# Router logits with Wr stationary in four column strips, the fourth Gram transpose as its own step, and batch 2's exponential and groups two or three places later

## The reference

```python
x = x + layernorm(attn(layernorm(x), Wqk, Wv, Wo, tau))
x = x + layernorm(ffn(layernorm(x), ln_g, ln_b, Wr, W1, W3, W2, W1s, W3s, W2s))
```

```python
logits = h @ Wr                                # h [8192, 256], Wr [256, 7]
top_vals, top_idx = jax.lax.top_k(logits, 2)
gates = jax.nn.softmax(top_vals, axis=-1)
# each token goes to its two experts, at most 732 places an expert, in order of tokens
routed = ...                                   # (silu(xe @ W1) * (xe @ W3)) @ W2, times the gate
shared = silu(h @ W1s) * (h @ W3s) @ W2s
```

## Time and profile before

| | |
|---|---|
| median of 3 runs | 1165.59 us |
| lowest and highest | 1161.06, 1172.66 us |
| the profiled execution | 1164.55 us |
| its span in the trace | 1162.8 us |
| TensorE busy | 1082.8 us, 93% |
| VectorE busy | 660.4 us, 57% |
| ScalarE busy | 506.2 us, 44% |
| GpSimd busy | 384.4 us, 33% |
| records of `u_route`'s products (line 1245) | 256 |

### The profile page before, as it was taken

One profiled execution on the slowest core, in us unless ns is written; L12 is line 12 of the kernel. 1 busy time (PEld: TensorE's weight loads), 2 busy tenths in 40 slices (PEclk: granted clock), 3 DMA queues, 4 the chain that ended last, 5 costly groups with the idle time before them and its releaser, 6 DMA issues.

```text
span 1162.8 us, 19459 instructions
## 1 busy us (share of the span) xinstructions
PE 1082.8 (93%) x6837; PEld 988.9 (85%) x6837; DVE 660.4 (57%) x1712; ACT 506.2 (44%) x887; POOL 384.4 (33%) x344
## 2 busy tenths in 40 slices
PE   6889889999989999869999889999999999999994
PEld 6877778998777898758898679999999999999873
DVE  6767555566844567744468423455453644546596
ACT  3334234343243343334344323546464554635385
POOL 3114360113460112450112561243353444311276
PEclk9989999999989999989999899999999999999998
DMA  9872360143350043352134230453241424315589
GB/s 306 326 250 98 121 199 2 37 142 122 119 182 19 19 143 134 106 182 73 37 109 129 105 104 17 156 124 102 63 138 35 135 55 116 82 14 158 201 192 218
DMA packets 83310, 141.44 MB, mean 122 GB/s; under 512 B 10389, under 2 KB 57625, under 8 KB 83233
## 3 DMA queue, kind: packets, MB, share of 16 engines
q1 hardware_dynamic: 64736, 105.11, 27.5%
q0 software_dynamic: 18496, 35.35, 12.9%
HBM read 73.72 MB, written 66.69 MB: 121 GB/s over the span
## 4 chain that ended last, share of the span: by engine, by line
PE 77%; DVE 8%; issue 5%; POOL 3%; ACT 2%; another core or an unknown queue 2%; DMA 1%; DVEq 0%; POOLq 0%; SPq 0%; ACTq 0%
PE bank L1115 23%; PE bank L1117 23%; PE bank L1116 23%; PE bank L1132 2%; POOL out_dram L890 2%; PE bank L1245 2%; POOL sb_t_scale L895 1%; PE bank L1234 1%; DVE sb_act_lo L1666 1%; PE bank L1277 1%; PE bank L1159 1%; DVE sb_act L1690 1%; DMA sb_ysb<-in_L_ffn_W2s_dram 1%; PE bank L1187 1%
## 5 line engine op out<-in xcount | busy, mean ns | idle before, releaser
L1690 DVE TENSOR_TENSOR sb_act<-bank,sb_act 128x512 f32<-128x512 f32 (+2 forms) x240 | 148.7, 620 | 397.2 <-PE bank L1117 301.0
L1115 PE MATMUL bank<-sb_h_hi,sb_wup_lo 128*128 128x512 f32 (+2 forms) x960 | 357.8, 373 | 8.0 <-ACT sb_act L1044 4.8
L1117 PE MATMUL bank<-sb_h_hi,sb_wup_hi 128*128 128x512 f32 (+2 forms) x960 | 352.5, 367 | 1.5 <-issue 1.5
L1116 PE MATMUL bank<-sb_h_lo,sb_wup_hi 128*128 128x512 f32 (+2 forms) x960 | 352.4, 367 | 0.0
L1044 ACT ACTIVATE sb_act<-bank 128x512 f32<-128x512 f32 (+2 forms) x240 | 129.8, 541 | 434.5 <-PE bank L1117 324.4
L1115 PE MATMUL bank<-sb_wdn_hi,sb_act_lo 128*128 128x256 f32 (+1 forms) x848 | 248.1, 293 | 17.4 <-DVE sb_act_lo L1666 10.5
L1116 PE MATMUL bank<-sb_wdn_lo,sb_act_hi 128*128 128x256 f32 (+1 forms) x848 | 240.0, 283 | 1.7 <-issue 1.7
L1117 PE MATMUL bank<-sb_wdn_hi,sb_act_hi 128*128 128x256 f32 (+1 forms) x848 | 240.5, 284 | 0.3 <-issue 0.3
L1115 PEld LDWEIGHTS bank<-sb_h_hi,sb_wup_lo 128*128 128x128 f32 x960 | 182.8, 190 | 27.8 <-ACT sb_act L1044 5.1
L1117 PEld LDWEIGHTS bank<-sb_h_hi,sb_wup_hi 128*128 128x128 f32 x960 | 182.3, 190 | 23.6 <-issue 0.5
L1116 PEld LDWEIGHTS bank<-sb_h_lo,sb_wup_hi 128*128 128x128 f32 x960 | 183.0, 191 | 18.5 <-issue 1.0
(11 more groups left out here) (248 smaller groups left out, 1289.0 us busy)
## 6 DMA issues: line engine op xcount, KB each, us to landing
sb_xin<-in_L_ffn_W_dram SPq DMA_DIRECT2D x28, 512.0 KB
sent_scratch<-sb_early SPq DMA_DIRECT2D x8, 1548.0 KB, 9.0
sb_x<-in_L_attn_x_dram SPq DMA_DIRECT2D x16, 512.0 KB
out_dram<-sb_x SPq DMA_DIRECT2D x16, 512.0 KB, 3.9
sb_xin<-in_L_attn_x_dram SPq DMA_DIRECT2D x14, 512.0 KB
sb_xin<-in_x_turned_dram SPq DMA_DIRECT2D x14, 512.0 KB, 4.1
y_scratch<-sb_ysb SPq DMA_DIRECT2D x14, 512.0 KB
sb_xn<-in_L_ffn_W_dram SPq DMA_DIRECT2D x14, 512.0 KB
```

Of the source, the lines that this page charges most:

```text
L1115: t_.matmul(o, a_lo, b_hi, start=start, stop=False, skip_group_check=True)
L1116: t_.matmul(o, a_hi, b_lo, start=False, stop=False, skip_group_check=True)
L1117: return t_.matmul(o, a_hi, b_hi, start=False, stop=stop, skip_group_check=True)
L1690: v.tensor_tensor(act[:, m % 2, 0:c.w], bank[(4 if c.wide and m % 2 else 0) + 1][:, 0:c.w], act[:, m % 2, 0:c.w], ALU.mult).then_inc(act_o ...
```

## The change

The logits: Wr is kept in 32 columns, 25 of them zero (a memset by POOL ahead of the other constants; SP's load of Wr waits for it). It is the stationary operand now, and h moves: for each half k of the channels and each of four strips of 32 output partitions, one product with 128 moving columns, the strip's 32 tokens of each of the group's 4 tiles. The result has experts on 32 partitions a strip, so VectorE's copy becomes a transpose in 32x32 blocks, into a tile `lgq` of 32 columns a token tile, of which `lg` is a view of 7.

The chain: the fourth transpose leaves `m_turn` for a step `m_cross` in the next place, together with `m_sym`; what follows moves one place. Batch 2's exponential moves three places, what is behind it with it, and its groups two (`MIX_AT` 107 in place of 105), with their routing and sends.

```diff
-        wr = sb("wr", [P, KC, E])
+        wr = sb("wr", [P, KC, QUAD])
...
-        lg = sb("lg", [P, 2 * GT, E])
+        lgq = sb("lgq", [P, 2 * GT, QUAD])
+        lg = lgq[:, :, 0:E]
...
-        logits = bank[7][:, 0:GT * 8].rearrange("p (t e) -> p t e", e=8)[:, :, 0:E]
+        turned_logits = bank[7][:, 0:GT * QUAD]
...
-        M_STEPS = ("m_gram", "m_turn", "m_sym", "m_times_wqk", ...
+        M_STEPS = ("m_gram", "m_turn", "m_cross", "m_sym", "m_times_wqk", ...
...
-        M_AT_PLACES = (0, 1, 1, 2, 2, 3, 3, 4, 5, 5, 6, 7, 8, 8, 9, 9, 10)
+        M_AT_PLACES = (None, (0, 1, 2, 2, 3, 3, 4, 4, 5, 6, 6, 7, 8, 9, 9, 10, 10, 11),
+                       (0, 1, 2, 2, 3, 3, 4, 4, 5, 6, 6, 9, 10, 11, 11, 12, 12, 13),
+                       (0, 1, 2, 2, 3, 3, 4, 4, 5, 6, 6, 7, 8, 9, 9, 10, 10, 11))
...
-        X_AT, MIX_AT = (None, 14, 72, 131), (None, 46, 105, 164)
+        X_AT, M_AT, MIX_AT = (None, 14, 72, 131), (None, 34, 93, 152), (None, 46, 107, 164)
...
-            put(b, MIX_AT[b] - 12, 0, zip(M_STEPS, M_AT_PLACES))
+            put(b, M_AT[b], 0, zip(M_STEPS, M_AT_PLACES[b]))
...
-            weight(wr, Wr, vec_in)
+            sp.wait_ge(const_ok, 1)
+            sp.dma_start(wr[:, :, 0:E], Wr.rearrange("(k p) n -> p k n", p=P)).then_inc(vec_in, 16)
...
+            made(v.memset(wr[:, :, :], 0.0))
...
                                      ident[:, :])
+
+            def m_cross(b, q):
+                if b > 0:
                     pe.wait_ge(m_chain, b * 9 + 1)
                 o = 0 if b == 0 else D
                 t_.transpose(bank[6][:, o:o + P], gf[:, 0, P:D], ident[:, :]).then_inc(m_pe, 1)
...
-                for t in range(GT):
-                    for k in range(KC):
-                        ins = t_.matmul(bank[7][:, t * 8:t * 8 + E], h[:, k, t * P:(t + 1) * P], wr[:, k, :],
+                for k in range(KC):
+                    for quad in range(0, P, QUAD):
+                        ins = t_.matmul(bank[7][quad:quad + QUAD, 0:GT * QUAD].rearrange("p (t r) -> p t r", r=QUAD),
+                                        wr[:, k, :],
+                                        h[:, k, :].rearrange("p (t r) -> p t r", r=P)[:, :, quad:quad + QUAD],
                                         start=(k == 0), stop=(k == KC - 1))
...
-                v.tensor_copy(lg[:, q % 2 * GT:(q % 2 + 1) * GT, :], logits).then_inc(lg_ok, 1)
+                v.transpose(lgq[:, q % 2 * GT:(q % 2 + 1) * GT, :].rearrange("p t r -> p (t r)"),
+                            turned_logits).then_inc(lg_ok, 1)
```

More of the change, by code:

```diff
@@ L73, in sandwich_kernel @@
     CLEAR = 4
+    QUAD = 32
     SENT_ROWS = 32 * SPARE * P
@@ L212, in sandwich_kernel @@
         blank = early[:, 0:SPARE * UW]
-        lg = sb("lg", [P, 2 * GT, E])
+        lgq = sb("lg", [P, 2 * GT, QUAD])
+        lg = lgq[:, :, 0:E]
         same = sb("same", [P, 2 * GT, E])
@@ L338, in sandwich_kernel @@
         t_out = [sem(f"t_out{i}") for i in range(TY)]
-        NCONST = 21
+        NCONST = 22
         H_LOADS = 16 * (GB - 1)
@@ L444, in sandwich_kernel @@
         T_STEPS = (("x_turned", (13, 16, 18, 20)), ("x_keep", (16, 18, 21, 23)), ("x_low", (17, 19, 22, 24)))
-        M_STEPS = ("m_gram", "m_turn", "m_sym", "m_times_wqk", "m_keep_t", "m_dots", "m_keep_s", "m_diag", "m_rowdiag",
+        M_STEPS = ("m_gram", "m_turn", "m_cross", "m_sym", "m_times_wqk", "m_keep_t", "m_dots", "m_keep_s", "m_diag", "m_rowdiag",
                    "m_logits", "m_exp", "m_softmax", "m_times_wo", "m_keep_n", "m_times_wv", "m_high", "m_low")
@@ L448, in sandwich_kernel @@
                       ("x_turned", (14, 14, 14, 15)), ("x_keep", (16, 18, 24, 26)), ("x_low", (19, 20, 34, 34)))
-        M_FIRST_AT = (20, 22, 23, 24, 25, 26, 27, 28, 30, 31, 32, 33, 34, 35, 36, 36, 37)
-        M_AT_PLACES = (0, 1, 1, 2, 2, 3, 3, 4, 5, 5, 6, 7, 8, 8, 9, 9, 10)
+        M_FIRST_AT = (20, 22, 22, 23, 24, 25, 26, 27, 28, 30, 31, 32, 33, 34, 35, 36, 36, 37)
+        M_AT_PLACES = (None, (0, 1, 2, 2, 3, 3, 4, 4, 5, 6, 6, 7, 8, 9, 9, 10, 10, 11),
+                       (0, 1, 2, 2, 3, 3, 4, 4, 5, 6, 6, 9, 10, 11, 11, 12, 12, 13),
+                       (0, 1, 2, 2, 3, 3, 4, 4, 5, 6, 6, 7, 8, 9, 9, 10, 10, 11))
         O_STEPS = (("o_mix", 0), ("o_stats", 1), ("o_norm", 3), ("o_apply", 3), ("o_add", 5), ("u_stats", 7),
@@ L1263, in u_count @@
                 ins.then_inc(r_cnt, 1)
-            steps = {"x_gram": x_gram, "m_turn": m_turn,
+            steps = {"x_gram": x_gram, "m_turn": m_turn, "m_cross": m_cross,
                      "m_times_wqk": m_times_wqk, "m_dots": m_dots, "m_rowdiag": m_rowdiag,
@@ L1585, in top @@
                 of_e = rank[:, :].rearrange("p (a e) -> p a e", a=1).broadcast_to([P, 2 * GT, E])
-                ch.link(v.tensor_reduce(best[:, c, :], lg[:, :, :], AX.X, ALU.max))
-                ch.link(v.tensor_tensor(same[:, :, :], lg[:, :, :], over_e(best[:, c, :]), ALU.is_equal))
+                ch.link(v.tensor_reduce(best[:, c, :], lg, AX.X, ALU.max))
+                ch.link(v.tensor_tensor(same[:, :, :], lg, over_e(best[:, c, :]), ALU.is_equal))
                 ch.link(v.tensor_tensor(same[:, :, :], same[:, :, :], of_e, ALU.mult))
@@ L1595, in r_top @@
                 ch.link(top(0, ch))
-                v.scalar_tensor_tensor(out=lg[:, :, :], in0=oh[:, :, 0, :], scalar=-BIG, in1=lg[:, :, :],
+                v.scalar_tensor_tensor(out=lg, in0=oh[:, :, 0, :], scalar=-BIG, in1=lg,
                                        op0=ALU.mult, op1=ALU.add).then_inc(r_top_ok, 1)
```

## The result

The changed kernel took 1157.68 us in the median of 21 runs (1147.87 to 1171.18). The kernel before, run beside it, took 1163.20 us (21 runs, 1157.01 to 1176.55). The ratio is 0.994, 95% interval 0.9912 to 0.9968: about 7 us gained, less than 1% (5.5 us by the two medians). The forecast's parts summed to 14.1 us gained, its time to 1150.0 us; the time lies in its range of 1138 to 1164. The profiled execution took 1158.23 us, its span 1156.5 us.

A forecast was written before the change was run, and what follows sets the result against it. TensorE was taken as the bound through the middle of batch 1, busy all of a 90 us stretch. 1164.55 - 6.0 (logits) - 4.2 (fourth transpose) - 3.9 (batch 2 later) = 1150.45, so 1150.0 us; range 1138 to 1164.

The forecast's parts named there:

- the wait ahead of batch 2's fourth transpose: Sign on TensorE: at most 3.5 us, with a down or an up between the third and fourth transpose.
- the waits ahead of the product with Wo: Sign at L1179: about 1 us in batches 1 and 3, none in batch 2.
- The logits: Router logits on TensorE: a group falls from 1.70 to 1.2 us, saving 0.5 us; 6.0 us gained in all.
- 16 records in 9 steps: Logits on TensorE: only a strip's second record overlaps the next strip's first, so the records take 0.9 us.
- The rival of full overlap: Logits: all four strips run at once, saving 1.3 us a group, 15.6 in all; around 1141 us, chance 0.15.
- Twelve groups by the step: Only batches 1 to 3's groups count, where TensorE is the bound: 12 x 0.5 = 6.0 us gained.
- VectorE's transpose: Replaces VectorE's copy of the logits: 0.28 us, 0.1 us more, 16 times, covered by VectorE's free time.
- The fourth transpose: Own step in the attention chain: 0.8 + 1.5 + 4.5 gained, 2.6 lost at L1179; 4.2 us gained.
- likely to stay at its place: Batch 1, VectorE ahead of L1453: the 7.07 us gap stays; a down fills TensorE's hole, 0.8 us gained.
- part 3: Batch 2's exponential three places later, groups two: L1179's 2.1 us wait goes, clock adds 0.9 twice; 3.9 us gained.
- the clock: Batch 2, TensorE around L1179: idle time also cost clock speed; 0.9 us gained twice.
- The sends: Rival: batch 2's moved sends put two more unreleased waits into batch 3's chain, 4 to 9 us; about 1157, chance 0.10.

The follow-up runs named there:

- gated_after: Changed kernel with POOL waiting for each send's place, so sends get pauses; 1119.10 us, 0.9626 of the kernel before.
- gated_p23: Changed kernel with the logits as before and POOL waiting for each send's place; 1128.47 us, 0.9708 of the kernel before.
- p2_cross: Kernel before with only the fourth transpose as its own step, in batches 1 to 3; 1145.82 us, ratio 0.9973.
- p3_later: Kernel before with only batch 2's exponential and groups moved later; 1145.28 us, ratio 1.0001.
- p23_chain: Changed kernel with the logits as before: fourth transpose's step and batch 2 later; 1153.24 us, 1.0049 of the kernel before.
- gated_before: Kernel before with POOL waiting for each send's place, so sends get pauses; 1127.90 us, 0.9714 of the kernel before.
- after_again: The changed kernel unaltered, run again on a second chip; 1155.78 us, 0.9987 of the kernel before.

## Why the prediction was right, and where it was not

The total fell into the range and on the right side, but that was luck: with the sends gated the logits give 9.4 us where 6.0 were forecast and the chain nothing where 8.1 were, and with the sends as they are even their sum is not steady (0.994, then 0.9987). Of the signs that it named, the logits step is below its 0.9 to 1.2 us and the wait ahead of batch 2's fourth transpose, 6.40 us, above its 3.5; the waits ahead of the product with Wo stand in batches 1 and 3 and not in 2, as it said, and VectorE's longest wait without a releaser, 10.0 us, stays under 11.22.

**The logits: right in kind, half the size.** Forecast 0.5 us a group, measured 1.0 us in TensorE's order and 9.4 us of time in place of 6.0. The step that failed is "16 records in 9 steps": that only the second record of a strip can overlap with the first of the next. The records say otherwise. Windows of the changed kernel on line 1255 alone (first the window and its length, then busy us and number of records active of PE and PEld):

```profile
430.80:430.83 0.03, 0.00 (x0) 0.00 (x0) 1.00 0.00 0
430.83:430.86 0.03, 0.03 (x4) 0.03 (x5) 1.00 0.00 0
...
430.92:430.95 0.03, 0.03 (x4) 0.03 (x8) 1.00 0.00 0
...
430.98:431.01 0.03, 0.03 (x8) 0.03 (x6) 1.00 0.00 0
...
431.04:431.10 0.06, 0.06 (x12) 0.06 (x8) 1.00 0.00 0
```

Four records start together, and the next four some 0.12 us later, about the 100 ns that one record of 128 columns takes in a row. So 16 records take four steps and not nine; which record goes to which strip, the trace doesn't show. The rival of full overlap had this right (1.3 us saved); the ends cost 0.27 us of it, close to the 0.3 us that I took. The Trainium skill ("TensorE: Matmul & The Clock Gate", Measured speedup vs the span model) had led to an estimate of 0.67 us a step, from a row for three strips; the trace has 0.67 us for four, but with the ends' 0.27 us in it, so that the two figures meet is partly chance. The row names no type, and that it isn't known to hold for float32 I let weigh more than it should.

**Twelve groups by the step: right as a rule, not in full.** 12 by 1.0 us is 12, the measured 9.4. gated_after has 14.0 us less TensorE work than gated_p23 (1058.3 against 1072.3 us busy), and 3.4 us more of its waits for VectorE's low parts (ten waits where there were four) and 1.5 us more for the silu. With less work on TensorE, the other two engines, which do the same work for each chunk, are late more often here.

**VectorE's transpose: right.** 0.30 to 0.32 us against 0.28 forecast; it ended no wait of TensorE.

**The fourth transpose: the mechanism right, the sizes wrong.** A down or an up stands ahead of it now in every batch, and the price at the product with Wo is 1.8 us each in batches 1 and 3 (forecast 1.3). But the waits of 4.64, 4.93 and 5.53 us that I meant to fill were mostly not the chain's. With the sends gated 0.38, 2.33 and 2.41 us of them are left in the unchanged kernel, each ahead of the fourth transpose. What I filled was mostly time in which VectorE and ScalarE stood still for late updates, and in the changed kernel's trace it wasn't filled: it came again, as 8.51 us behind batch 1's fourth transpose and 6.40 us ahead of batch 2's. I had read the gap of 7.07 us as "likely to stay at its place"; it was a clue that the wait had another cause, and I drew only one batch's sum from it. Forecast 4.2 us gained, measured with part 3 together nothing.

**Batch 2 later: the wait went, another came.** The product with Wo of batch 2 no longer waits, as forecast (2.11 us), though one place would have done, as p2_cross shows. What I had at nothing were the groups behind it. Their places moved by two, so four normalisations by ScalarE now stand ahead of the copy of a chunk's result. Timeline of ACT of the changed kernel:

```profile
412.53 1.93 ACT L953 ACTIVATE sb_ln_o<-bank,sb_nbiasB,sb_rstdB 128x256 f32<-128x256 f32 x4 [3.79 <-DVE sb_nbiasB L1526]
414.34 1.10 ACT L1032 ACTIVATE sb_ysb<-bank 128x512 f32<-128x512 f32 x2
```

TensorE waits for that copy at 415.58, 2.39 us. The same 2.4 us stand in p3_later, p23_chain and all the gated kernels with part 3. In gated_before the same four normalisations are followed by a silu, and the copy comes behind it without a wait of TensorE. The 1.8 us that I took for the clock no run sizes by itself. The step that failed is that I asked only what the sends and SP meet at their new places, and not what ScalarE's own work meets.

**The sends: the right suspect, too small a part.** The rival had two more waits fall into batch 3's chain, 4 to 9 us. They stood in every batch, gating the sends took some 35 us off the kernel before (1162.95 to 1127.90), and most of the spread of the runs went with it. What spoke for it stood in the earlier trace rows: VectorE's longest wait ends at 519.11, 2.1 us behind the end of batch 2's last send. Nor is the chain the one place where TensorE stands still: the kernel before also waits 3.99 us at 124.21, 2.78 at 480.94 and 2.69 at 682.55, each in a run of sends or within 2 us behind one. I had read "remote" as a gap that keeps its place, and not asked whose semaphore it was.

**What stays open.** The runs show what holds the updates of TensorE (an unbroken run of sends) and that pauses free them, not by what path in the chip. Gating also moves most sends to later times; apart from batch 2's two places in p3_later, which gained nothing, no run does that without breaking their runs. Whether a short pause without a wait for a place would do in batch 3's two runs of sends, and whether the strips overlap as well when both products of a strip are issued one behind the other, was not tried.

## What to carry to other kernels

Before filling a wait, follow the semaphore that ended it to the instruction that should have raised it; if that instruction was long done, the wait belongs to whatever delays the update, and moving work into it gained nothing here. Try a pause after each two to four of a long run of indirect DMAs by POOL, and only then size other changes: here it was worth four times the change itself, and the spread of the runs fell from 21 us to between 3 and 8 us. When a group of steps is moved, look at each engine's order at the new places, its plain copies too.

## What was not expected of the hardware

- TensorE's semaphore updates come up to 10 us late in the first traces of the two kernels (22 us in that of after_again) while POOL issues rows to DRAM by indirect DMAs back to back (0.96 us each, 0.30 us between), and mostly its matmuls go on; 17 of 167 are late in the first two sends of a run, 147 of 173 from the ninth. VectorE's and ScalarE's were not in the changed kernel's trace (0 of 971), nor TensorE's beside gathers and accumulating scatters, which come in threes (0 of 146).
- Products of 128 by 32 in float32 into four strips of output partitions run side by side: 16 records in 0.58 us, in four fours.
